# The masked layer of a top-k feed-forward kernel, written into a second buffer before its check is read

## The reference

```python
x = layernorm(x + x @ (W + delta_W).T)
z = x @ ternary_quant(W_syn).T + b_syn            # 2048 wide
thresh = top_k(z, 204)[0][:, -1:]                 # the 204th largest of each row
hidden = where(z >= thresh, relu(z), 0.0)
out = hidden @ ternary_quant(W_out).T + b_out
y = layernorm(x + layernorm(x + out) * gamma + beta)
```

## Time and profile before

| | |
|---|---|
| median of 3 runs | 645.19 us (644.47 to 648.13) |
| the profiled execution's own time | 646.16 us |
| its span in the profile | 644.4 us |
| TensorE busy | 591.5 us, 92% |
| VectorE busy | 549.6 us, 85% |
| ScalarE busy | 550.8 us, 85% |
| GpSimd busy | 373.4 us, 58% |
| mean granted TensorE clock | 0.966 of full |

### The profile page before, as it was taken

The page is one execution under the profiler, slowest core; times in us unless marked ns, Lnnn a source line. Parts: engine busy times, 40 slices in busy tenths (PEclk is TensorE's granted clock), DMA queues, the critical chain, the costliest instruction groups (busy, mean ns, idle before and its releaser), DMA issues. The chain is left out here.

```text
span 644.4 us, 8560 instructions
## 1 busy us (share of the span) xinstructions
PE 591.5 (92%) x2482; PEld 267.4 (41%) x2482; DVE 549.6 (85%) x657; ACT 550.8 (85%) x724; POOL 373.4 (58%) x712
## 2 busy tenths in 40 slices
PE   8799779899999999999999999999999999896473
PEld 6434324344444444444444444444444444342121
DVE  4796997999888998898899988899889889988772
ACT  0797558999999999999999999999999999978832
POOL 0126286665655666666666565566666666655562
PEclk9999679999999999999999999999999999989888
DMA  8981234546555453556563655535355554453342
GB/s 320 322 255 50 49 82 83 113 84 132 98 92 114 84 114 81 123 99 131 99 132 82 130 99 101 107 81 113 81 125 99 100 98 98 82 99 82 64 74 76
DMA packets 184579, 71.65 MB, mean 111 GB/s; under 512 B 168144, under 2 KB 176336, under 8 KB 183888
## 3 DMA queue, kind: packets, MB, share of 16 engines
q1 hardware_dynamic: 184528, 71.07, 50.3%
HBM read 20.72 MB, written 8.39 MB: 45 GB/s over the span
## 5 line engine op out<-in xcount | busy, mean ns | idle before, releaser
L539 ACT ACTIVATE junk<-z_sb,t_col 128x2048 f16<-128x2048 f32 x128 | 254.9, 1992 | 9.1 <-POOL t_col L436 8.1
L954 PE MATMUL z_ps<-t_syn,xhT 128*128 128x512 f16 x1024 | 231.0, 379 | 2.7 <-DVE t_syn L660 2.7
L954 PEld LDWEIGHTS z_ps<-t_syn,xhT 128*128 128x128 f16 x1024 | 99.8, 98 | 134.5 <-issue 18.3
L967 PE MATMUL o_ps<-t_out,hT 128*128 128x512 f16 x512 | 123.9, 399 | 17.9 <-DMA hT<-hh 14.3
L417 POOL TENSOR_SCALAR tmp<-signs,dev 128x1 f32<-128x1 f32 x64 | 45.4, 710 | 152.1 <-ACT junk L539 152.1
L937 PE MATMUL u_ps<-weff,xT_sb 128*128 128x512 f32 x256 | 118.6, 607 | 3.2 <-ACT x1s L558 2.4
L974 PE MATMUL o_ps<-t_out,hT 128*128 128x512 f16 x512 | 119.0, 387 | 0.0
L832 DVE SCALAR_TENSOR_TENSOR z_sb<-z_sb,thr 128x2048 f32<-128x2048 f32 (+1 forms) x33 | 75.4, 2287 | 28.2 <-DVE flag L810 26.7
L576 ACT ACTIVATE hh<-z_sb,sc 128x2048 f16<-128x2048 f32 (+1 forms) x33 | 64.3, 1951 | 30.1 <-DVE z_sb L832 30.1
L967 PEld LDWEIGHTS o_ps<-t_out,hT 128*128 128x128 f16 x512 | 51.8, 102 | 85.4 <-issue 26.6
L761 DVE SCALAR_TENSOR_TENSOR hh<-z_sb,sc,hh 128x2048 f16<-128x2048 f32 (+1 forms) x33 | 75.4, 2287 | 13.5 <-ACT hh L576 13.5
(11 more groups left out here) (118 smaller groups left out, 586.2 us busy)
## 6 DMA issues: line engine op xcount, KB each, us to landing
xT_sb<-in_xT SPq DMA_DIRECT2D x16, 512.0 KB, 4.7
out_y<-y_sb SPq DMA_DIRECT2D x32, 256.0 KB, 2.8
z_sb<-in_w_synT SPq DMA_DIRECT2D x4, 1024.0 KB, 13.7
hh<-in_w_outT SPq DMA_DIRECT2D x2, 1024.0 KB, 9.8
z_sb<-in_w_outT SPq DMA_DIRECT2D x2, 1024.0 KB, 10.4
hT<-hh SPq DMA_TRANSPOSE x66, 4.4
weff<-in_wT SPq DMA_DIRECT2D x2, 512.0 KB, 4.9
w_sb<-in_dwT SPq DMA_DIRECT2D x2, 512.0 KB, 6.3
```

Source lines behind the costliest of these rows:

```text
L539: a_.activation(junk[:, n % 2, :], z_sb[:, t % ZS, :], ACT.Sign, bias=at, scale=-1.0, accum_out=signs[:, j, r:r + 1]).then_inc(counted, 1)
L954: last = mm(z_ps[:, c, b * BANK:(b + 1) * BANK], xhT[:, j, h * KD + k, :], t_syn[:, k, n0:n0 + BANK], start=k == 0 and h == 0, stop=k == K ...
L967: mm(o_ps[t % OS][:, :], hT[:, j, 0, c, :], t_out[:, c, :], start=c == 0, stop=False)
```

## The change

`hidden` moves ahead of `general` and writes `w_sb` instead of `z_sb`, so the mask doesn't wait for the flag any more. `hi_h` and `lo_h` read `w_sb`. `general` follows; where its branch is taken, it waits until the high half is done, finds the threshold, and makes the masked layer and the high half again. At its end it counts up a new semaphore `h_checked`, for which SyncE's transpose of the high half waits. `below` waits for the low half of the tile before, since `w_sb` is now read by it. As z is no longer overwritten, `evac` waits for `h_made` instead of `h_lo` before it reuses a slot.

```diff
+        h_checked = sem("h_checked")
...
             def transpose_hi(t):
                 j = t % 2
+                sp.wait_ge(h_checked, t + 1)
...
-                    a_.activation(hh[:, t % 2, 0, cut], z_sb[:, t % ZS, cut], ACT.Copy, scale=sc[:, 6:7]).then_inc(h_hi, 1)
+                    a_.activation(hh[:, t % 2, 0, cut], w_sb[:, cut], ACT.Copy, scale=sc[:, 6:7]).then_inc(h_hi, 1)
...
-                    v.scalar_tensor_tensor(hh[:, j, 1, cut], z_sb[:, t % ZS, cut], sc[:, 6:7], hh[:, j, 0, cut], ALU.mult,
+                    v.scalar_tensor_tensor(hh[:, j, 1, cut], w_sb[:, cut], sc[:, 6:7], hh[:, j, 0, cut], ALU.mult,
                                            ALU.subtract).then_inc(h_lo, 1)
...
             def below(t):
                 dve.wait_ge(updated[-1], t + 1)
                 wait(dve, max8_done, t)
+                wait(dve, h_lo, t)
...
                 if c == 0:
-                    wait(dve, h_lo, t - ZS + 1)
+                    wait(dve, h_made, t - ZS + 1)
...
+            def hidden(t):
+
+                dve.wait_ge(thr_made, 2 * t + 2)
+                for cut in parts(t):
+                    z = z_sb[:, t % ZS, cut]
+                    v.scalar_tensor_tensor(w_sb[:, cut], z, thr[:, t % 2:t % 2 + 1], z, ALU.is_ge, ALU.mult).then_inc(h_made, 1)
+
             def general(t):
...
                 with dve.If(good != P):
-                    v.tensor_copy(w_sb[:, :], z_sb[:, t % ZS, :])
+                    dve.wait_ge(h_hi, t + len(parts(t)))
+                    dve.drain()
+                    v.tensor_copy(w_sb[:, :], z)
...
                     dve.drain()
-
-            def hidden(t):
-                dve.wait_ge(thr_made, 2 * t + 2)
-                for cut in parts(t):
-                    z = z_sb[:, t % ZS, cut]
-                    v.scalar_tensor_tensor(z, z, thr[:, t % 2:t % 2 + 1], z, ALU.is_ge, ALU.mult).then_inc(h_made, 1)
+                    v.scalar_tensor_tensor(w_sb[:, :], z, thr[:, j:j + 1], z, ALU.is_ge, ALU.mult)
+                    dve.drain()
+                    v.tensor_scalar(hh[:, j, 0, :], w_sb[:, :], sc[:, 6:7], None, ALU.mult)
+                    dve.drain()
+                dve.sem_inc(h_checked, 1)
...
+            hidden(0)
             general(0)
-            hidden(0)
...
                 if live(f):
+                    hidden(f)
                     general(f)
-                    hidden(f)
```

More of the change, by code:

```diff
@@ L804, in lo_x @@
                 v.tensor_tensor(xh[:, j, 1, :], x1s[:, t % XS, :], xh[:, j, 0, :], ALU.subtract).then_inc(x_lo, 1)
+            def hidden(t):
[3 more added lines that the diff above has]
+                    v.scalar_tensor_tensor(w_sb[:, cut], z, thr[:, t % 2:t % 2 + 1], z, ALU.is_ge, ALU.mult).then_inc(h_made, 1)
             def general(t):
                 j = t % 2
+                z = z_sb[:, t % ZS, :]
                 dve.wait_ge(flag_ready, t + 1)
```

## The result

The changed kernel takes 639.87 us (638.74 to 640.14), the kernel before beside it 646.26 us (644.47 to 648.13), four executions each: ratio 0.9902, 95% interval 0.9874 to 0.993. It is faster by 6.4 us. A second timing of the same two gave 639.82 against 645.70, again 0.9902.

What follows compares the result with a forecast made beforehand. TensorE was taken as the bound, busy 419.33 of 419.40 us in the middle. Gains 1.8 + 1.1 + 1.6 + 0.4 + 0.9 = 5.8, less 0.5, gave 5.3 us: 645.19 becomes 639.9, range 638.2 to 643.0.

Steps and rivals of the forecast that it cites:

- The middle is worth nothing: Middle tiles: TensorE keeps its 17.47 us per tile, so the shorter VectorE loop gains 0 there.
- Buffer, waits and increment at nothing: Writing w_sb and the changed waits cost 0; the extra semaphore increment on VectorE was taken as 0.1 us.
- Filling, 1.8 us: First tiles: the earlier mask cuts TensorE's 2.90 us wait to 1.1, moving its whole middle 1.8 us earlier.
- Lead into the emptying, 1.1 us: End of the middle: VectorE runs ahead until an evac waits for TensorE, entering the emptying 1.1 us earlier.
- The slack of `flag_read`, 0.8 us in the middle: TensorE's second z block: the later flag copy leaves 0.8 us to spare, 0.3 where `ok` comes last; cost 0.
- The first emptying turn, 1.6 us: First turn of `below` in the emptying: full clock after a 1.7 us wait, 18.64 becomes 16.95; 1.6 us kept.
- Second and third turn, 0.4 and 0.9: Later emptying turns: second falls from 17.3 to 16.95, saving 0.4 us; third, without evacs, saves 0.9.
- Last tile, 0: Last tile: h_checked comes 4.2 us behind `ok`, so the transpose goes as late as before; gain 0.
- The deduction of 0.5: Emptying: the next flag wait grows from 1.50 to about 2.8 us and may drop the clock; 0.5 us deducted.
- Rival B: Emptying: waits of 1.7 and 2.8 us still lower TensorE's clock, losing 1.6 and perhaps 0.4; 642.1 us, chance 0.14.
- Rival C: Emptying: longer branch body costs 2.6 us, late h_checked or evac takes the 1.1 lead; 643.6 us, chance 0.08.
- Rival D: Middle: flag_read comes too late for TensorE in some 25 tiles, 0.8 us each; slower, 660 us, chance 0.05.

Runs made afterwards that it cites:

- buffer only: Kernel before with the masked layer written into w_sb and the new semaphores and waits, flag and branch still ahead of the mask in every tile: 646.65 us, ratio 1.0008.
- tiles 3 to 27: Changed kernel with the mask ahead of the flag in tiles 3 to 27 only, the old order elsewhere: 645.41 us, ratio 0.9995 to the kernel before.
- tiles 28 to 31: Changed kernel with the mask ahead of the flag in tiles 28 to 31 only, the old order elsewhere: 645.04 us, ratio 0.9983 to the kernel before.
- tiles 0 to 2: Changed kernel with the mask ahead of the flag in tiles 0 to 2 only, the old order elsewhere: 643.38 us, ratio 0.9965 to the kernel before.
- flag behind the first evac: Changed kernel with flag copy and branch of tiles 3 to 27 moved behind add_v and the first evac: 641.56 us, ratio 0.9934 to the kernel before.
- no branch at the end: Changed kernel with the flag copied but not branched on in tiles 28 to 31, fallback search left out there: 638.18 us, ratio 0.9878 to the kernel before.
- split only: Changed kernel with the last tile's flag copied and branched on between the two halves of its mask, no waits filled: 639.58 us, ratio 0.9901 to the kernel before.
- flag behind the low half: Changed kernel with flag copy and branch of tiles 3 to 27 moved behind the low half: 719.3 us, ratio 1.1131 to the kernel before.

## Why the prediction came out, step by step

- **The middle is worth nothing: right.** Same period, 419.25 of 419.30 us busy. The freed time is idle at evac and first count. What it buys unseen is cover for long branches, which cost up to 1 us in the old order.
- **Buffer, waits and increment at nothing: right**, 1.0008 with these alone, to 0.2%. The longer body, also taken as 0, may not be quite that: the kernel before has one long branch, at tile 0, and every kernel with the new body has several. That the body's length makes them isn't shown.
- **Filling, 1.8 us: right**, 1.70 in the stretch that was worked out. Another 0.37 comes from tile 0, between the first two flag products (24.3 us with the old order there, 23.9 with the new, in every profile), which the sum left out. The wait expected at 1.1 is 1.21, and 1.18 when the filling alone is changed. Not foreseen: the old wait of 2.90 could itself drop the clock. That shows in no term of the sum, and its filling brought about 1 us.
- **Lead into the emptying, 1.1 us: right**, 1.26 in the profile. The evac at 550.82 stands 7.24 us behind the flag product, as worked out (3.58 + 3.65).
- **The slack of `flag_read`, 0.8 us in the middle: too small**, since the lead was left out of it. In the kernel after the copy ends at 300.32 and the z block starts at 302.55, 2.2 us later; at tile 3, where 0.3 was worked out, it is 0.5. Both leave the term at 0.
- **The first emptying turn, 1.6 us: the size is near the profile's 1.46, the reason was wrong.** The step that failed is "with 1.1 us off the wait is 1.7 us ... then the turn is what the loops allow", as far as it takes 18.64 for what a wait of 2.87 gives. After waits of 3.06 and 2.17 us in the old order the clock stayed, and the turns were 17.72 with a long branch and 17.43 without. So the new order gives 17.43 - 17.18 = 0.25 us, and the other 1.21 us are the deep fall of the clock in that one execution. In the kernel before with the filled wait it fell at this place too, but less deep (the block took 5.17 us), and the turn was 17.42.
- **Second and third turn, 0.4 and 0.9: too large**, 0.22 and 0.66. The branch takes 1.05 us between copy and add_v where the two parts of 0.86 and 0.1 were taken. It took 1.43 in the third turn, but the same kernel without it also has 16.62 there, so it isn't what holds that turn. The mask is early enough, but ScalarE's count at 598.77 then waits 0.17 for `t_col` of the round before: the loop over GpSimd takes back part of what the mask had given. Timeline of ScalarE there, kernel after:

```profile
598.77 2.00 ACT L541 ACTIVATE junk<-z_sb,t_col 128x2048 f16<-128x2048 f32 x1 [0.17 <-POOL t_col L438]
```

- **Last tile, 0: right, and the reason shown.** The transpose goes 4.16 us behind `ok` (4.2 predicted); without the branch 3.33.
- **The deduction of 0.5: the event right, the size too large.** The next flag wait grew to 2.98 and the clock fell to 0.70; the evac behind it waited 0.32 us, 0.58 in the second profile of this kernel. The turn was 17.09 and 17.30, where with filled waits and no fall it was 17.07: 0.0 and 0.2 us.

Rival B (clock still falls) is out where its price lay: 1.00 behind the wait of 1.60. Its other half came true, a fall behind the wait of 2.98, and cost next to nothing. (Its 642.1 also takes the 0.5 off twice.) The section HAM oscillation (the Trainium skill, TensorE: Matmul & The Clock Gate), which was to speak for B, describes a kernel whose clock falls in each round of burst and wait, with waits of some 3 to 5 us; here the trace agrees only in part, since waits of 2.2 to 3.1 us went both ways and none of 1.8 us or less brought a slow block (the table at the end). Rival C (the longer body) shows in the long branches, far below its price. Rival D (flag read too late) is a real mechanism at the place named; the changed kernel is on the safe side of it, and two moves further it costs 80 us. Rival E (the loop bounds the middle) is out: the period stayed at 17.47.

The time itself, 639.9 against 639.87, is closer than its parts deserve, and that is luck. The sum was 5.3 us and the gain 6.4 (5.9 in the second timing), and the prediction started from 645.19, where the kernel before later gave 645.58 to 646.26: two misses of 1.1 us that cancel.

**Open:** the parts don't add up to the whole by their medians: 2.6 us (filling), 0.5 and 0.9 make 4.0, against some 6. Each of these differences is uncertain by about 1.3 us. From the first flag product to the end of the span, the profiles give 575.5 us with the buffer alone, 573.2, 574.3 and 575.9 for the three parts, and 569.3 for the whole (569.6 in its second profile). So the whole gains 6.2 us and the parts 2.3, 1.2 and -0.4. The fall of 1.7 us at 127 put back makes their sum 4.9, and the last high block of the middle's kernel (5.80 us, 5.14 with the buffer alone) 5.6. What is left, 0.3 to 0.6 us, is assigned to nothing but 0.1 of long branches at tile 28. How large the lead and the emptying are each, as a mean over executions, stays open.

## What to carry to other kernels

When the bound engine has no gap in the middle, a shorter loop beside it pays only in filling and emptying: count the turns there, and look at what becomes late next, as the branch did at the last tile and again when it was split. Before a slow stretch of the clock in one profile goes into a sum, look for the same wait in other executions: it may be a chance in each, with an average price. Products that nothing reads, put into such waits, were worth 2.0 us here beside the reordering. Compare turns only after looking at how long each branch took: 0.3 us of a long one looked like the change's own gain. An instruction off the bound can still cost its length by moving a VectorE instruction over a GpSimd one.

## What the hardware showed that was not expected

The clock's falls after equal waits. The waits are those ahead of a flag product, unfilled, one from each profile; in brackets the time of the block behind it, 16 products of 512 columns, where it wasn't 3.63 us, its time at 1.00.

| place | block behind it in 3.63 us | slow block behind it |
|---|---|---|
| tile 3 | 2.90 (before), 2.91 (buffer only), 2.90 (tiles 3 to 27) | 2.90 (tiles 28 to 31: 5.31) |
| tile 28 | 3.06 (buffer only), 2.17 (tiles 0 to 2), 3.08 (tiles 28 to 31) | 2.87 (before: 6.55), 2.87 (before, wait of tile 3 filled: 5.17) |
| tile 29 | 2.95 (buffer only), 2.45 (flag behind the first evac) | 2.34 (tiles 0 to 2: 5.31), 2.98 (tiles 3 to 27: 4.95), 2.55 (tiles 28 to 31: 5.31), 2.98 and 2.49 (after, two profiles: 5.06, 5.31), 2.20 (no branch at the end: 5.31), 2.96 (split only: 4.95), 2.98 (flag behind the low half: 5.25) |

The length of the wait doesn't tell which way it goes: 3.06 and 3.08 left the clock alone, 2.20 didn't. The place does tell something: a slow block in one of four at tile 3, two of five at tile 28, eight of ten at tile 29. Why isn't shown. No slow block followed a wait of 1.76 us or less ahead of a flag product in z, at any tile.

A branch that isn't taken has no single price. From the flag's copy to the next VectorE instruction it took 0.86 us in the old order and 1.05 in the new, and at some tiles 0.3 to 0.4 more. In six profiles with the new order throughout the long ones in the middle stand at the same four tiles, 4, 12, 17 and 25, so they go with the place in the program and not with the execution; what makes them isn't shown.

And a GpSimd step on one column, 0.27 us by itself, took 1.08 us under a VectorE instruction with two SBUF inputs.
